# A recurrent two-layer fp32 kernel on one core: projections, feed forward and running sums issued at other ticks, the second pause of each gap two ticks later, normed keys on one engine

## The reference

```python
xn = layernorm(x)
s = causal_softmax_attention(xn)              # 16 heads of 64: xn @ Wq, Wk, Wv, softmax, @ Wo + bo
g = silu(shared_ffn(xn) + routed_experts(xn)) # each of 8 experts takes its top token (K = 1) of all tokens
x = x + s * g
xn = layernorm(x)
s = linear_attention(xn)   # phi = elu + 1; k v products and k summed along the tokens (cumsum), 16 heads of 8
g = silu(L1_ffn(xn))       # two layers, each:
                           #   h = shift_token(x); q, k, v = h @ wqkv; q, k divided by their norms, rotated
                           #   x = x + windowed softmax attention (8 heads of 64, window 64) @ wo
                           #   x = x + a * gelu(g) @ w2 + b2,  a, g from layernorm(shift_token(x)) @ w1 + b1
x = x + s * g
```

## Time and profile before

| | value |
|---|---|
| median of three runs | 2111.61 us |
| span of the profiled execution | 2112.1 us |
| profiled execution's own time | 2113.86 us |
| PE busy | 1783.7 us, 84% |
| DVE busy | 1255.7 us, 59% |
| ACT busy | 1187.6 us, 56% |
| POOL busy | 895.2 us, 42% |
| steady period of 36 ticks | 234 us |

### The profile page before, as it was taken

One profiled execution on the slowest core, in us unless ns is written; L12 is line 12 of the kernel. 1 busy time (PEld: TensorE's weight loads), 2 busy tenths in 40 slices (PEclk: granted clock), 3 DMA queues, 4 the chain that ended last, 5 costly groups with the idle time before them and its releaser, 6 DMA issues.

```text
span 2112.1 us, 38035 instructions
## 1 busy us (share of the span) xinstructions
PE 1783.7 (84%) x12532; PEld 1147.1 (54%) x12532; DVE 1255.7 (59%) x4179; ACT 1187.6 (56%) x3527; POOL 895.2 (42%) x1025
## 2 busy tenths in 40 slices
PE   6679989997989889987989889987989798685876
PEld 4358754663565456654465456554565455363554
DVE  4434447556666556656766556656766656867653
ACT  2444547655656665666666565566566565553643
POOL 2633216523643245423553255414653255647510
PEclk9889999999999989999999999999999997787978
DMA  8146500000000000000000000000000000000000
GB/s 234 45 157 208 189 16 5 8 1 1 6 2 16 1 1 6 17 1 1 6 1 16 1 1 7 16 1 1 6 2 11 1 6 1 1 6 0 1 1 11
DMA packets 49725, 53.49 MB, mean 25 GB/s; under 512 B 6386, under 2 KB 42236, under 8 KB 49532
## 3 DMA queue, kind: packets, MB, share of 16 engines
q0 software_dynamic: 7808, 27.79, 4.0%
q1 hardware_dynamic: 41724, 23.26, 3.9%
HBM read 41.60 MB, written 9.44 MB: 24 GB/s over the span
## 4 chain that ended last, share of the span: by engine, by line
PE 46%; DVE 12%; issue 10%; ACT 7%; POOL 7%; DVEq 0%; ACTq 0%; POOLq 0%
PE ps L650 5%; PE ps L608 4%; PE ps L588 4%; PE ps L547 4%; PE ps L725 3%; PE ps L567 3%; PE ps L632 3%; PE ps L767 2%; PE ps L776 2%; PE ps L769 2%; PE ps L622 2%; POOL xn L308 2%; POOL big L1447 2%; DVE p L1033 2%; POOL big L1446 1%
## 5 line engine op out<-in xcount | busy, mean ns | idle before, releaser
L1333 POOL COPY rdx<-rden 128x256 f32<-128x256 f32 x256 | 99.5, 418 | 599.9 <-DVE rden L1050 574.9
L1033 DVE CUSTOM_DVE_ANT_0 p<-ps,mask 128x128 f32<-128x128 f32 (+1 forms) x512 | 152.2, 353 | 249.8 <-PE ps L580 215.3
L1033 DVE CUSTOM_DVE_ANT_0 p<-ps,mask,nrq 128x128 f32<-128x128 f32 x512 | 149.0, 347 | 204.1 <-PE ps L576 203.4
L588 PE MATMUL ps<-ident,p 128*128 128x128 f32 x1280 | 221.4, 297 | 26.8 <-ACT p L865 23.9
L865 ACT ACTIVATE p<-p,nmax 128x128 f32<-128x128 f32 (+1 forms) x512 | 226.4, 442 | 0.0
L725 PE MATMUL ps<-wqkv,hT 128*128 128x512 f32 x384 | 197.4, 623 | 27.9 <-ACT big L944 27.7
L864 ACT ACTIVATE p<-p,nmax 128x128 f32<-128x128 f32 x512 | 200.3, 391 | 34.5 <-DVE nmax L1033 34.0
L879 ACT ACTIVATE pt<-ps 128x384 f32<-128x384 f32 (+1 forms) x256 | 111.7, 436 | 185.2 <-PE ps L588 184.6
L588 PEld LDWEIGHTS ps<-ident,p 128*128 128x128 f32 x1280 | 143.8, 147 | 107.0 <-issue 89.2
L1446 POOL TENSOR_TENSOR big<-big,rots 128x512 f32<-128x512 f32 x64 | 99.6, 1556 | 206.0 <-ACT big L944 206.0
L557 PE MATMUL ps<-ident,big 128*128 128x128 f32 x512 | 90.9, 317 | 93.3 <-DVE big L1228 47.6
(11 more groups left out here) (251 smaller groups left out, 4207.7 us busy)
## 6 DMA issues: line engine op xcount, KB each, us to landing
slots_in<-xn SPq DMA_DIRECT2D x1, 2560.0 KB, 14.0
v<-slots_in SPq DMA_DIRECT2D x20, 128.0 KB, 4.6
slots_out<-v SPq DMA_DIRECT2D x20, 128.0 KB, 1.9
big<-in_x SPq DMA_DIRECT2D x4, 512.0 KB, 6.1
x<-in_x SPq DMA_DIRECT2D x8, 256.0 KB, 3.0
out_x<-x SPq DMA_DIRECT2D x8, 256.0 KB, 2.3
wqkv<-in_wqkv SPq DMA_DIRECT2D x2, 768.0 KB
xn<-in_x SPq DMA_DIRECT2D x6, 256.0 KB, 3.2
```

The lines of the kernel that those rows point to most:

```text
L588: last = nc.tensor.transpose(bank[:, j * P:(j + 1) * P], c.p[:, u % 4, j * P:(j + 1) * P], c.ident[:, :])
L1033: last = V.tensor_tensor_reduce(out=c.p[:, u % 4, a:b], in0=bank[:, a:b], in1=mask, scale=scale, scalar=3e38, op0=ALU.add, op1=ALU.min, ac ...
```

## The change

The second pause of each gap moves from 12, 13 to 14, 15 of the 18 ticks; the pair of kind 0 that stood there comes two ticks earlier. `v` becomes a segment of one tile. For blocks from the fourth on (b >= 3; `XRING` is 3) the first half of `v` goes 11 ticks ahead of the block's first kind-0 step, which is the second tick of the moved pause of the gap before it; the second half is split in two tiles two ticks ahead and two tiles seven ticks after that step (before: all four five ticks after). `xload`, `xn`, `xnT` of these blocks go to 19, 18 and 15 ticks ahead (before: 5, 4 and 3). The planner's rule for `ffn`, `r`, `down0` and `comb` is unchanged, but with `xload` gone from where it stood it now finds a place five ticks earlier for b = 2 to 6 (`ffn` at ticks 145 to 147 instead of 150 to 152, for instance); b = 1 and 7 stay. In the running sums `cum` 2 and 3 of the first sequence and their `sum` go two ticks later, `kv` of tiles 2 and 3 one tick later, in all eight blocks. `kn` is done by DVE for all four tiles.

```diff
-            self.fill(18, (8, 9, 12, 13))
+            self.fill(18, (8, 9, 14, 15))
...
-            for t, at in enumerate((-1, 0, 6, 7)):
+            for t, at in enumerate((-1, 0, 7, 8)):
                 self.put(l0 + at, "kv", b, t)
             for n in range(2 * LPARTS):
-                at = l0 + 1 + n + 4 * (n >= LPARTS)
+                at = l0 + 1 + n + 2 * (n >= 2) + 2 * (n >= LPARTS)
                 self.put(at, "cum", b, n // LPARTS, n % LPARTS)
                 self.put(at + 1, "sum", b, n // LPARTS, n % LPARTS)
...
-        held, shared = [(self.first[(0, b, 0, 0)] - 5, self.first[(0, b, 0, 0)] - 3) for b in range(2, BLOCKS)], {}
+        held, shared = [], {}
+        for b in range(2, BLOCKS):
+            f0 = self.first[(0, b, 0, 0)]
+            held.append((f0 - 5, f0 - 3) if b < XRING else (f0 - 19, f0 - 15))
         for b in range(BLOCKS):
             f0, f1 = self.first[(0, b, 0, 0)], self.first[(0, b, 1, 0)]
             if b >= 2:
-                self.put(f0 - 5, "xload", b)
-                self.put(f0 - 4, "xn", b)
-                self.put(f0 - 3, "xnT", b)
-                assert f0 - 3 > shared[b - 2], b
-            if b:
-                self.put(f0 - 2, "v", b, 0)
-            self.put(f1 - 3, "v", b, 1)
+                x0, x1 = held[b - 2]
+                self.put(x0, "xload", b)
+                self.put(x0 + 1, "xn", b)
+                self.put(x1, "xnT", b)
+                assert x1 > shared[b - 2], b
+            for t in range(TILES):
+                if b:
+                    self.put(f0 - (2 if b < XRING else 11), "v", b, 0, t)
+                self.put(f1 - 3 if b < XRING else f0 - 2 if t < 2 else f0 + 7, "v", b, 1, t)
...
-    def values_of_tokens(b, half):
-        for t in range(TILES):
-            bank = mm_bank("v", b, half, t)
-            MM(bank[:, :], c.xnT[:, b % 2, t * P:(t + 1) * P], c.wv[:, half * 512:(half + 1) * 512],
-               start=True, stop=True).then_inc(c.mm_full, 1)
+    def values_of_tokens(b, half, t):
+        bank = mm_bank("v", b, half, t, 0)
+        MM(bank[:, :], c.xnT[:, b % 2, t * P:(t + 1) * P], c.wv[:, half * 512:(half + 1) * 512],
+           start=True, stop=True).then_inc(c.mm_full, 1)
...
         dve.wait_ge(c.rot_ready, TILES * (g + 1))
-        for t in range(KN_VECTOR):
+        for t in range(TILES):
             k_over_norm(V, c, t).then_inc(c.kn_ready, 1)
...
-        for t in range(KN_VECTOR, TILES):
-            k_over_norm(G, c, t).then_inc(c.kn_ready, 1)
```

More of the change, by code:

```diff
@@ L44 @@
 RSQRT_MAGIC = 1597463007.0
-KN_VECTOR = 2
 class Common:
@@ L460, in count_units @@
     for t in range(TILES):
-        mm.add(("v", 0, 0, t))
+        mm.add(("v", 0, 0, t, 0))
     mm.add(("q", 0))
@@ L595, in values @@
             if st.i == 0:
-                pe.wait_ge(c.mm_done, mm.done("qkv", st.b, st.part, END, 2) if st.kind else mm.done("v", st.b, st.part, END))
+                pe.wait_ge(c.mm_done, mm.done("qkv", st.b, st.part, END, 2) if st.kind else mm.done("v", st.b, st.part, END, 0))
         v = c.v1[:, plan.turn[(st.b, st.part)] % 2, :, :] if st.kind else c.v0[:, st.part, :, :]
@@ L638, in xnT, with v @@
         to_features(bank, c.xn0)
-    def v(b, half):
+    def v(b, half, t):
         pe.wait_ge(c.mm_done, mm.done("rT", b) if b < 2 else mm.done("xnT", b, 0))
-        values_of_tokens(b, half)
+        values_of_tokens(b, half, t)
     def wo(kind, b, part):
@@ L809, in tensor @@
     pe.wait_ge(c.wqk_loaded, 16 * 3)
-    values_of_tokens(0, 0)
+    for t in range(TILES):
+        values_of_tokens(0, 0, t)
     produce(0, plan.step(0))
@@ L847, in shifted, with values_of_tokens @@
         A(two(c.hT[HD:P, :])[:, :, 1:SEQ], two(bank[HD:P, :])[:, :, 0:SEQ - 1], ACT.Copy).then_inc(c.mm_done, 1)
-    def values_of_tokens(b, half):
-        for t in range(TILES):
-            evacuate(c.v0[:, half, t, :], "v", b, half, t)
+    def values_of_tokens(b, half, t):
+        evacuate(c.v0[:, half, t, :], "v", b, half, t, 0)
     def produce(which, st):
@@ L1461, in gpsimd @@
     stage = {"scatter": scatter, "wg": wg, "r": r, "xn": xn, "tables": tables, "lin": lin, "kv": kv, "qkv": qkv,
-             "kn": kn, "shift": shift, "cum": cum, "ln1n": ln1n}
+             "shift": shift, "cum": cum, "ln1n": ln1n}
     pool.memset(c.zero[:, 0, :], 0.0).then_inc(c.zero_ready, 1)
```

## The result

| | before | changed |
|---|---|---|
| median | 2112.3 us | 2142.66 us (2141.41 to 2143.76) |
| ratio of the comparison | | 1.0144, interval 1.0126 to 1.0161 |
| span | 2112.1 us | 2142.0 us |
| PE busy | 1783.7 | 1796.3 |
| DVE busy | 1255.7 | 1290.2 |

The kernel became slower by 30 us where 5 us less was forecast, and the time lies outside the range. 2112.3 us is the kernel before, run again beside the changed one.

The account below looks back on a forecast made before the run. PE, busy 84%, was taken as the bound, through its waits and half-clock work. Five periods −4.0, first block +4.6, sixth gap −0.8 and tail −4.5 made −4.7 us: 2107 us, range 2082 to 2127.

Parts of the forecast that it names:

- F: Tick 128: POOL's fourth-tile product, now behind the expansion, makes PE wait 3.1 us, plus 1.5 for the clock: +4.6 us.
- Rival one: Slower: the new wait of F decides, at 6.5 us in each of seven or eight places; about 2120 us, chance 0.22.
- the tail: End of the kernel: PE's 9.3 us wait for the keys shortens as POOL's product goes later; −4.5 us.
- E: Ticks 120 to 127: shorter wait for the layer norm, against sums and values work added on PE; +1.5 us.
- The clock: Low clock around PE's waits: extra cost of 1.7 us after the shorter wait, up to 3.4 with the longer.
- C: Tick 149 to the k produce of tick 154: work and a wait leave, a new 2.0 us wait comes; −9.4 us.
- A: Gap's end, tick 137 to the k produce: one wait instead of two, added values projections cost nothing; −0.2 us.
- B: Transpose xT to tick 149: the feed forward's three chunks and down0 come in; +6.4 us.
- D: Tick 130: four values projections leave a PE that doesn't wait there; −3.7 us.
- Rival two: Faster: F is only 2.5 us and C gives 11; −5.0 a period, thus 2084 us, chance 0.22.
- Rival three: Slower: masked steps and scaling delay DVE's keys, +2 us in six gaps and the tail; 2116 to 2121, chance 0.10.
- Rival four: Nothing comes of it: C gives 8.5 us, a period is +0.1; about 2111 us, chance 0.13.

## Why the prediction was wrong, step by step

The step that failed is **F**, together with what the sum left out because of it. Its mechanism was right: product behind the expansion, addition ending near 888.1 in the old times, PE waiting from 884.86. Forecast +4.6 a place; measured +6.8. Two things were missing. POOL's two operations take 2.66 and 2.94 us, not the 2.22 and 2.62 of the earlier trace rows, since DVE's `fin` lies beside them; that makes the wait 3.95 instead of 3.1. And the low clock behind it lasts 6.8 us (row 899.40 above), where I had taken the 3.4 of the shorter case. It also missed DVE's own chain through `fin` and the mask, which by itself holds 4.3 of the 6.8 and hides in the time of the other. Rival one had this price, 6.5, and its sign came true (a mean clock of 0.92 in the period, under 0.94); it forecast 2120, as it kept the rest of the sum.

The sum had F six times, 27.6 us, and took the tail's own as cancelled. The traces have it at six places with 5.9 to 6.9 and at a seventh, in the tail, with 7.1, and the ticks of the sums cost 40 us in all. The other terms fell short too. The sum without F came to some −32 us; the run with the sums at their old ticks is at −10 by the ratio and at −15 between the traces, so the rest gave less than half of what it was down for. Its four periods from tick 83 on came out at −2.1 to −4.5, where the terms without F said −5.4 (1.0 of the difference is E's, as the wait for the layer norm grows back), and its tail at +2.4 instead of −4.5.

**The tail** was the second failure, −4.5 forecast and +8.5 measured. I took POOL's product away from the keys and let the roots lose their POOL neighbour, which had lengthened only one of their operations. The order shows the opposite: `cum` 2 and 3 and both products now stand beside the roots. The bound of +4.0 was for the keys; the neighbour fell on the roots instead, thirteen small dependent operations, which went from 5.2 us to 12.9.

**The clock** was the third. It was priced at the wait that causes it, but the changed kernel has 46 low stretches of 378 us in all against 41 of 332. The rise of 2.1 us behind C's new wait, in five blocks, is 11 us that the sum didn't have, and most of it (1.5 to 1.8 a block) stays with the sums at their old ticks. The one at tick 134 stands at a wait that didn't change.

**A** came out right in sign and a little larger (−1.1): one wait of 4.82 us instead of 5.34 and 3.10. But the credit isn't the keys'. Over the same ticks the pause alone gives −2.5, pause and keys −1.6, and with the moved work it is −1.1: DVE's four tiles (2.49 us, forecast 2.58) end later than two engines would, and the four values projections, which I had costed at nothing, take up to 0.5. **B**, by the precedent in the same trace, was +6.4 forecast, and its stretch took 30.8 us as said; the +7.2 of the table holds the ticks ahead of it too, with a wait for the norm of the tokens that grew from 1.59 to 2.90. **C** was −9.4 forecast, −9.2 measured to the k produce; the new wait behind the roots is 3.6 rather than 2.0, and PE's busy time fell by 10.5 instead of 9.5. **D** was −3.7, measured −3.5. **E** was +1.5, measured +1.1; the wait for the layer norm fell to 2.99 for the 2.7 expected.

Rival two (no wait at tick 128) fell by the new group in PE's waits. Rival three (late keys) fell in the gaps and holds in the tail, where the keys are late because of the roots. Rival four fell.

The Trainium skill's page "SBUF — State Buffer", section "Who interferes with whom", gives the rule that a DVE instruction with two SBUF inputs and a GpSimd instruction that reads SBUF exclude each other. I applied it to the keys and to the old neighbours only. The traces agree with it at three new places (fin 0.69 to 2.98, the roots' 0.23 to 2.65, POOL's addition 2.62 to 2.94). Every long POOL operation that moves should have been laid beside DVE's new neighbours.

## What to carry to other kernels

Before an engine that works in order gets a long operation one slot later, list two things: who waits for it, and what the engine that such operations were seen to lengthen does in that slot. Either can hold the critical engine alone, and taking one away may show nothing until the other goes too. The rest of a schedule change can be worth having while one part of it costs four times as much, and one line alone can give all of the gain: try the parts apart. Look also at what stands ahead of a critical operation on its own engine, as the expansion did ahead of POOL's keys.

## What the runs showed of the hardware that was not expected

A chain of small dependent DVE operations suffered much beside long POOL operations: the thirteen of the roots, 0.2 us each, took 12.9 us in all beside `cum` and `kv`, four times their 3.2. And the clock behind one and the same wait differed within one kernel. In the kernel before, ticks 131 to 137 and their like in the next blocks have the same waits of PE (0.8 us for a mask, then 2.8 for the layer norm). From 902.6 and from 1373.6 us they ran at full clock throughout and took 36.2 us; from 666.8, 1137.4 and 1608.4 us they had a low stretch of 6.8 us and took 38.4 to 38.7. In the changed kernel five of six blocks have the low stretch. What decides between the two, no run here separates, so a price of the clock by the wait alone was uncertain here by about 2.2 us a place.
